# Two masked cross attentions: the masks are made inside the projection block, the mask transfers are issued first, and the position vectors are padded to 128 rows

## The chip, the cores and the metric

One Trainium2 chip, one of its cores. The metric is the device time of one execution of the whole program in microseconds (us). TensorE does matrix products, VectorE (DVE), ScalarE (ACT) and GpSimd (POOL) do elementwise work, SyncE (SP) issues the transfers (DMAs). TensorE's clock has two levels, 1.2 and 2.4 GHz; the profile shows which was granted (0.50 or 1.00).

## The reference

A post-norm decoder of four layers on x of shape (4, 256, 128), thirteen stages one after the other, each followed by `x = layernorm(x + stage(x))`. Two of the stages matter here. Both are cross attentions with 16 heads of 8 features; queries come from x, keys and values from `ctx` (4 x 256 x 128).

```python
# stage L1_xattn: an additive mask
qh, kh, vh = split(x @ wq.T + bq), split(ctx @ wk.T + bk), split(ctx @ wv.T + bv)
score = einsum('bhqd,bhkd->bhqk', qh, kh) / sqrt(8) + mask * -1e9
out = softmax(score) @ vh, heads joined;  return out @ wo.T + bo

# stage L2_xattn: position vectors beside the features, a bias over distance, a boolean mask
sym = (arange(256) % 2)[:, None] * Wsym                   # (256, 64), the same for all batches
query = concat([x, sym], -1) @ Wq + bq                    # 128 + 64 features in
key, value = concat([ctx, sym], -1) @ Wk + bk, concat([ctx, sym], -1) @ Wv + bv
bias = distance_scale * log1p(dist) + parity_strength * (1 - 2 * parity) - dist / exp(localization_length)
logits = where(mask, (query . key + bias) / sqrt(8), finfo.min)
return (softmax(logits) @ value) @ Wo + bo
```

## The kernel before

Activations lie transposed: 128 features in the partitions, 1024 tokens (4 batches of 256) in the free direction, in float32. `decoder` runs the thirteen stages in order.
A masked cross attention is five pieces of work:

1. A mask block. SP fetches the mask and its transpose. In `L1_xattn` DVE scales `mask` by -1e9, ACT scales `maskT`, and POOL clears the buffers `v_heads` and `shiftsT` (`clear_head_buffers`). In `L2_xattn` the pack is waited for and the next pack issued in a block of its own (`weights_in`); then, in the mask block, SP fetches the byte masks `keep` and `keepT`, ACT makes `near`, and DVE makes `sym`, the `bias` (four operations in a chain), and out of the byte masks and the bias `mask` and `maskT`.
2. The projections, `stream(...)`. It takes a list of jobs; job j is a group of products into PSUM bank j modulo 8 on TensorE, and an evacuation by DVE or ACT. A job waits for a free bank only from the ninth on; here there are six. `head_jobs` makes two jobs (two halves of 512 tokens) for q, evacuated by DVE, and two for k, by ACT; `value_jobs` makes two of four 128 x 128 products each, by DVE. In `L2_xattn` each product is followed by a second one that adds `sym` times the `_sym` part of the weights, over 64 rows (partitions), into the same bank.
3. `attention8`, the core: ACT and DVE split q and k in bfloat16 parts, DMAs lay them out by head, TensorE makes scores, and so on. Masks are read here and nowhere earlier.
4. The output product with `add_and_norm`.

A float32 product shows in the trace as two MATMUL records, called pieces here. Line 146 is the product in `stream`, 838 the evacuation of q, 1361 that of k, 1373 that of v, 71 the transfer of a pack.

Of the kernel before, what the change touches and what calls it, by code (L numbers as in the profile page):

```python
# [20 lines left out]
ACT = mybir.ActivationFunctionType  # L21
ALU = mybir.AluOpType
AX = mybir.AxisListType

P = 128
# [95 lines left out]
def stream(K, tag, jobs, banks=8):  # L121
# [9 lines left out]
    with ExitStack() as stack:  # L131
# [18 lines left out]
        @block.scalar  # L150
        def _(act):
            for j, (eng, _, _, evacuate) in enumerate(jobs):
                if eng == "act":
                    act.wait_ge(product_done, j + 1)
                    evacuate(K.bank[j % banks]).then_inc(taken["act"], 1)

        @block.vector
        def _(dve):

            K.chain = Chain(dve, sem("dve_own"))  # L160
            for j, (eng, _, _, evacuate) in enumerate(jobs):
                if eng == "dve":
                    dve.wait_ge(product_done, j + 1)
                    evacuate(K.bank[j % banks]).then_inc(taken["dve"], 1)
# [1213 lines left out]
def L1_xattn(K):  # L1378
# [4 lines left out]
    with ExitStack() as stack:  # L1383
# [5 lines left out]
        with ExitStack() as inner:  # L1389
            sem = Sems(nc, inner, "L1_xattn_mask")  # L1390
            mask_in, cleared = sem("in"), sem("cleared")
            block = inner.enter_context(nc.Block())

            @block.sync
            def _(sp):
                sp.dma_start(mask[:], K.dram["mask_added"]).then_inc(mask_in, 16)
                sp.dma_start(maskT[:], K.dram["mask_addedT"]).then_inc(mask_in, 16)
                weights_wait(K, sp, "L1_xattn")

            @block.gpsimd  # L1400
            def _(pool):
                clear_head_buffers(K, pool, cleared)

            @block.vector
            def _(dve):
                dve.wait_ge(mask_in, 32)
                nc.vector.tensor_scalar(mask[:], mask[:], -1e9, None, ALU.mult)

            @block.scalar
            def _(act):  # L1410
                act.wait_ge(mask_in, 32)
                nc.scalar.activation(maskT[:], maskT[:], ACT.Copy, scale=-1e9)
        group = lambda w, src: lambda g, h: [(W(w)[:, g * P:(g + 1) * P], halves(src)[h])]
        stream(K, "L1_xattn_qkv",
               interleave(head_jobs(K, group("wq", x), W("bq"), q, 1 / math.sqrt(DH8)),
                          head_jobs(K, group("wk", ctx), W("bk"), k, 1.0, "act"))
               + value_jobs(K, lambda c: [(ctx[:, c * P:(c + 1) * P], W("wv"))], W("bv"), v))
# [199 lines left out]
def L2_xattn(K):  # L1617

    nc, x, ctx = K.nc, K.x, K.ctx
    weights_in(K, "L2_xattn")  # L1620
    W = lambda n: K.w("L2_xattn." + n)
    FH = P // 2
    with ExitStack() as stack:
# [7 lines left out]
        sym = sb("sym", [FH, 2 * S])  # L1631
        with ExitStack() as inner:
            sem = Sems(nc, inner, "L2_xattn_mask")
            mask_in, near_done, own = sem("mask_in"), sem("near_done"), sem("dve_own")
            block = inner.enter_context(nc.Block())

            @block.sync
            def _(sp):
                sp.dma_start(keep[:], K.dram["mask_kept"]).then_inc(mask_in, 16)
                sp.dma_start(keepT[:], K.dram["mask_keptT"]).then_inc(mask_in, 16)  # L1640

            @block.scalar
            def _(act):

# [3 lines left out]
            def _(dve):  # L1648
                chain = Chain(dve, own)
                bf = bias[:].rearrange("p c s -> p (c s)")  # L1650
                nc.vector.tensor_scalar(sym[:], W("odd"), W("wsym"), None, ALU.mult)
                chain.link(nc.vector.tensor_scalar(bf, W("log_distance"), W("distance_scale"), None, ALU.mult))
                chain.link(nc.vector.scalar_tensor_tensor(out=bf, in0=W("parity"), scalar=W("parity_strength"), in1=bf,
                                                          op0=ALU.mult, op1=ALU.add))
                dve.wait_ge(near_done, 1)

                chain.link(nc.vector.scalar_tensor_tensor(out=bf, in0=W("distance"), scalar=near[:], in1=bf,
                                                          op0=ALU.mult, op1=ALU.add))
                chain.link(nc.vector.tensor_scalar(bf, bf, 1 / math.sqrt(DH8), None, ALU.mult))
                dve.wait_ge(mask_in, 32)  # L1660

                for m, kept in ((mask, keep), (maskT, keepT)):
                    chain.link(nc.vector.tensor_scalar(m[:], kept[:], 1.0, -MASKED, ALU.subtract, ALU.mult))
                    for b in range(B):
                        mb = m[:, 2 * b:2 * b + 2, :]
                        nc.vector.tensor_tensor(mb, mb, bias[:], ALU.add)
        def group(w, src):
# [3 lines left out]
               interleave(head_jobs(K, group("wq", x), W("bq"), q, 1 / math.sqrt(DH8)),  # L1671
                          head_jobs(K, group("wk", ctx), W("bk"), k, 1.0, "act"))
               + value_jobs(K, lambda c: [(ctx[:, c * P:(c + 1) * P], W("wv")),
                                          (sym[:, (c % 2) * P:(c % 2 + 1) * P], W("wv_sym"))], W("bv"), v))
# [603 lines left out]

def parameters(i):
# [47 lines left out]
    for n in "qk":  # L2327
        w = i["L2_xattn_W" + n][:, by_depth]
        p["L2_xattn.w" + n], p[f"L2_xattn.w{n}_sym"] = w[:P], w[P:]
        p["L2_xattn.b" + n] = column(i["L2_xattn_b" + n][by_depth])  # L2330
    p["L2_xattn.wv"], p["L2_xattn.wv_sym"] = i["L2_xattn_Wv"][:P], i["L2_xattn_Wv"][P:]
    p["L2_xattn.bv"], p["L2_xattn.wo"], p["L2_xattn.bo"] = rows(i["L2_xattn_bv"]), i["L2_xattn_Wo"], column(i["L2_xattn_bo"])
    p["L2_xattn.wsym"] = column(i["L2_xattn_Wsym"])
# [50 lines left out]
    p["L2_xattn.odd"] = np.broadcast_to(np.tile(pos % 2, 2).astype(np.float32), (P // 2, 2 * S))  # L2384
# [43 lines left out]
```

## Time and profile before

| | |
|---|---|
| median of 3 runs | 1736.21 us (1733.26 to 1736.88) |
| the profiled execution | 1738.16 us, its span 1736.3 us |
| mean granted TensorE clock | 0.854 |
| TensorE busy | 1259.2 us, 73% of the span |
| DVE, ACT, POOL busy | 1009.3, 885.4 and 499.7 us |
| stage L1_xattn, first mask transfer to last evacuation of v | 611.98 to 630.48 us |
| stage L2_xattn, next pack's issue to last evacuation of v | 885.31 to 932.20 us |

The profiled execution's own time is 1.9 us above its span (start and end of the program around it). Times inside the trace count from the span's start.

### The profile page before, as it was taken

The page shows a single profiled execution, that of the slowest core. Times are in us where ns is not written, and L with a number is a line of the kernel's source. Part 1 is how long each engine was busy: PE and PEld are TensorE (multiplying, and loading weights), DVE is VectorE, ACT ScalarE, POOL GpSimd, SP SyncE. Part 2 cuts the span into 40 slices and gives each one's busy share as a digit, 9 for nine tenths or more (in the row PEclk, how much of TensorE's full clock was granted, in tenths as well). Part 3 has the DMA queues.
Part 4 walks back from the last instruction along what each step waited for, and adds up shares of the span by engine and source line. Part 5 has one row for each costly group of instructions (what it writes and reads, how often), then busy time and mean ns, then how long its engine had stood idle before and what let it go on. Part 6 is the DMA issues. An engine that isn't in the chain of part 4 may idle for free. (4 is left out here: it accounts for less than half of the span.)

```text
span 1736.3 us, 21579 instructions
## 1 busy us (share of the span) xinstructions
PE 1259.2 (73%) x7168; PEld 628.1 (36%) x7168; DVE 1009.3 (58%) x2042; ACT 885.4 (51%) x1822; POOL 499.7 (29%) x583
## 2 busy tenths in 40 slices
PE   6998645266666749866537996973985979888896
PEld 2575421022222215522213553431433434543462
DVE  2573456999999536413833644442734748736852
ACT  2673234599999546743013772231652564743653
POOL 0362002388888531100302210000200213422440
PEclk9999866589999978978865997975887799989998
DMA  3000000000000034011023400014411500000000
GB/s 136 2 2 2 19 8 0 1 0 0 0 1 0 0 112 90 2 43 37 0 79 66 81 2 35 0 31 107 92 51 37 110 13 39 1 1 1 0 2 13
DMA packets 43486, 52.73 MB, mean 30 GB/s; under 512 B 2800, under 2 KB 39792, under 8 KB 41968
## 3 DMA queue, kind: packets, MB, share of 16 engines
q1 hardware_dynamic: 43376, 51.35, 11.4%
q8 instruction: 58, 0.95, 0.2%
q14 instruction: 52, 0.43, 0.1%
HBM read 36.66 MB, written 14.68 MB: 30 GB/s over the span
## 5 line engine op out<-in xcount | busy, mean ns | idle before, releaser
L1341 POOL TENSOR_TENSOR L_attn_z<-L_attn_state,L_attn_r 128x1024 f32<-128x1024 f32 x64 | 150.8, 2358 | 40.0 <-DVE L_attn_state L1327 33.5
L1327 DVE TENSOR_TENSOR_SCAN L_attn_state<-bank,L_attn_w 128x512 f32<-128x512 f32 x128 | 149.0, 1205 | 0.0
L1238 PE MATMUL bank<-L_attn_z,const 128*128 128x512 f32 x256 | 138.1, 667 | 1.4 <-POOL L_attn_z L1345 1.4
L791 DVE CUSTOM_DVE_ANT_0 L_xattn_core_logits<-bank,L_xattn_mask 128x256 f32<-128x256 f32 x256 | 98.6, 422 | 53.9 <-PE bank L574 41.4
L146 PE MATMUL bank<-x,weights 128*128 128x512 f32 (+1 forms) x108 | 60.0, 711 | 59.6 <-PEq L181 26.1
L1222 PE MATMUL bank<-L_attn_rows,L_attn_select 128*128 128x512 bf16 x96 | 36.9, 442 | 86.1 <-ACT L_attn_C L1290 43.2
L1278 ACT ACTIVATE L_attn_r<-L_attn_after_dt,L_attn_half_guard,L_attn_A 128x512 f32<-128x512 f32 x128 | 96.5, 802 | 0.0
L1268 ACT ACTIVATE bank<-L_attn_dt,L_attn_A 128x510 f32<-128x510 f32 x128 | 86.5, 676 | 13.3 <-DVE L_attn_state L1327 13.3
L703 ACT ACTIVATE L_xattn_core_probs<-bank 128x512 f32<-128x512 f32 x132 | 71.5, 596 | 36.9 <-PE bank L617 25.5
L574 PE MATMUL bank<-L_xattn_core_rows 48*128 48x256 bf16 x384 | 64.6, 312 | 32.2 <-DMA L_xattn_core_rows<-L_xattn_core_slots 18.0
L1345 POOL TENSOR_TENSOR L_attn_z<-L_attn_z,L_attn_C 128x1024 f32<-128x1024 f32 x32 | 75.7, 2367 | 23.7 <-ACT L_attn_C L1290 23.6
L1308 DVE TENSOR_TENSOR L_attn_w<-bank,L_attn_udt 128x1024 f32<-128x1024 f32 x64 | 78.2, 1222 | 5.6 <-PE bank L1222 1.9
L411 POOL TENSOR_TENSOR L_attn_core_probs<-L_attn_core_probs,L_attn_core_rsum 128x256 f32<-128x256 f32 x64 | 51.5, 826 | 93.2 <-DVE L_attn_core_rsum L380 93.2
L1238 PEld LDWEIGHTS bank<-L_attn_z,const 128*128 128x128 f32 x256 | 54.2, 212 | 50.6 <-issue 39.7
L1284 ACT ACTIVATE L_attn_r<-L_attn_r 128x1024 f32<-128x1024 f32 x64 | 66.7, 1043 | 0.0
L2072 PE MATMUL bank<-L_ffn_shifted,weights 128*128 128x512 f32 x128 | 59.1, 606 | 10.0 <-PEq L1999 10.0
L411 POOL TENSOR_TENSOR L_ffn_core_probs<-L_ffn_core_probs,L_ffn_core_rsum 128x256 f32<-128x256 f32 x64 | 51.5, 826 | 45.5 <-DVE L_ffn_core_rsum L380 45.4
L2158 POOL TENSOR_TENSOR L_ffn_part<-L_ffn_part 128x512 f32<-128x512 f32 x32 | 40.8, 1274 | 59.4 <-DVE L_ffn_part L2137 59.4
L761 POOL TENSOR_TENSOR shiftsT<-L_xattn_core_top,nothing 128x8 bf16<-128x8 f32 x48 | 12.0, 251 | 157.6 <-DVE L_xattn_core_top L791 104.6
L602 PE MATMUL bank<-L_xattn_core_rows 48*128 48x256 bf16 x384 | 56.8, 284 | 0.4
L345 ACT ACTIVATE L_ffn_core_probs<-bank,L_ffn_core_negmax 128x128 f32<-128x128 f32 (+1 forms) x128 | 52.0, 426 | 9.2 <-DVE L_ffn_core_negmax L371 9.2
L607 PE MATMUL bank<-L_xattn_core_shifts,minus_rows 48*128 48x256 bf16 x384 | 56.6, 283 | 0.0
(466 smaller groups left out, 3029.9 us busy)
## 6 DMA issues: line engine op xcount, KB each, us to landing
L_xattn_core_rows<-L_xattn_core_slots SPq DMA_DIRECT2D x24, 384.0 KB, 5.8
weights<-in_pack_L_ffn SPq DMA_DIRECT2D x2, 2118.5 KB, 7.9
L_xattn_core_slots<-L_xattn_core_k_parts SPq DMA_DIRECT2D x24, 128.0 KB, 2.0
L_attn_core_rows<-L_attn_core_slots SPq DMA_DIRECT2D x8, 384.0 KB, 5.5
weights<-in_pack_L_ffn SPq DMA_DIRECT2D x1, 2824.0 KB, 9.4
weights<-in_pack_L_attn SPq DMA_DIRECT2D x1, 2304.0 KB, 8.5
L_xattn_core_slots<-L_xattn_core_q_parts SPq DMA_DIRECT2D x12, 192.0 KB, 2.2
weights<-in_pack_L_xattn SPq DMA_DIRECT2D x1, 1539.5 KB, 6.2
```

The lines of the kernel that those rows point to most:

```text
L411: last = nc.gpsimd.tensor_tensor(part, part, rsum[:, i % NB, :, sc:sc + 1].to_broadcast([P, 2, keys[sc].stop]), ALU.mult)
L574: last = nc.tensor.matmul(scores_bank[side][:, c * S:(c + 1) * S], row(QUERIES, side, p, c), row(KEYS, side, p), start=True, stop=True)
L703: nc.scalar.activation(probs[n % 3][:, at], shifted_bank[at][:], ACT.Exp).then_inc(exp_done, 1)
L791: last = nc.vector.tensor_tensor_reduce(logits[:, c], scores_bank[side][:, c * S:(c + 1) * S], mask[:, 2 * b + c, :], 1.0, MASKED, ALU.add ...
L1238: last = nc.tensor.matmul(y_bank[2 * c + half][:], ident, z[:, g % NS, c], start=False, stop=False, skip_group_check=True)
L1268: nc.scalar.activation(two(a_bank[c][:])[:, :, lo:lo + S - 1], two(dt[d][:, c, tokens(half)])[:, :, lo:lo + S - 1], ACT.Exp, scale=A[d][:, ...
L1278: last = nc.scalar.activation(r[:, g % NS, c], after_dt[d][:, c, tokens(half)], ACT.Tanh, bias=half_guard[:], scale=A[d][:, 1, at:at + 1])
L1284: nc.scalar.activation(r[:, g % NS], r[:, g % NS], ACT.Copy, scale=0.5, bias=0.5).then_inc(r_done, 1)
L1308: nc.vector.tensor_tensor(w[:, g % 2], B_bank[:].unsqueeze(1).to_broadcast([P, DC, HALF]), udt[d][:, :, tokens(half)], ALU.mult).then_inc( ...
L1327: nc.vector.tensor_tensor_scan(state[:, g % NS, c, ::step], a_bank[c][:, ::step], w[:, g % 2, c, ::step], 0.0, ALU.mult, ALU.add).then_inc ...
L1341: nc.gpsimd.tensor_tensor(z[:, g % NS], state[:, g % NS], r[:, g % NS], ALU.mult).then_inc(z_done, 1)
L1345: nc.gpsimd.tensor_tensor(z[:, g % NS], z[:, g % NS], copied[:, g // 2 % 2].unsqueeze(1).to_broadcast([P, DC, HALF]), ALU.mult).then_inc(p ...
```

## The change

In `stream` there are three new arguments: `dve_first` puts work at the head of DVE's list of the block, `act_last` at the end of ACT's, `on_pool` gives POOL a list. The scaling of the masks and the clearing of buffers (`L1_xattn`), and the bias and the masks (`L2_xattn`), move there. What is left ahead of the projections in `L1_xattn` is a block in which SP issues three transfers. In `L2_xattn` there are two: one in which SP issues `keep`, `keepT` and then the next stage's pack, and one in which ACT makes `near` and DVE `sym`. In both stages the jobs of k come ahead of those of q. `sym` and the `_sym` weights have 128 rows, of which the upper 64 hold zeros; the packs were already stored with 128 rows, so they keep their sizes.

```diff
-def stream(K, tag, jobs, banks=8):
+def stream(K, tag, jobs, banks=8, dve_first=None, act_last=None, on_pool=None):
...
                     evacuate(K.bank[j % banks]).then_inc(taken["act"], 1)
+            if act_last:
+                act_last(act)
+
+        if on_pool:
+            @block.gpsimd
+            def _(pool):
+                on_pool(pool)
 
         @block.vector
         def _(dve):
 
             K.chain = Chain(dve, sem("dve_own"))
+            if dve_first:
+                dve_first(dve)
             for j, (eng, _, _, evacuate) in enumerate(jobs):
...
 L1_xattn:
-        with ExitStack() as inner:
-            sem = Sems(nc, inner, "L1_xattn_mask")
-            mask_in, cleared = sem("in"), sem("cleared")
-            block = inner.enter_context(nc.Block())
-
+        sem = Sems(nc, stack, "L1_xattn_mask")
+        mask_in, cleared = sem("in"), sem("cleared")
+        with nc.Block() as block:
             @block.sync
             def _(sp):
                 sp.dma_start(mask[:], K.dram["mask_added"]).then_inc(mask_in, 16)
                 sp.dma_start(maskT[:], K.dram["mask_addedT"]).then_inc(mask_in, 16)
                 weights_wait(K, sp, "L1_xattn")
 
-            @block.gpsimd
-            def _(pool):
-                clear_head_buffers(K, pool, cleared)
-
-            @block.vector
-            def _(dve):
-                dve.wait_ge(mask_in, 32)
-                nc.vector.tensor_scalar(mask[:], mask[:], -1e9, None, ALU.mult)
-
-            @block.scalar
-            def _(act):
-                act.wait_ge(mask_in, 32)
-                nc.scalar.activation(maskT[:], maskT[:], ACT.Copy, scale=-1e9)
+        def scale_mask(dve):
+            dve.wait_ge(mask_in, 32)
+            nc.vector.tensor_scalar(mask[:], mask[:], -1e9, None, ALU.mult)
+
+        def scale_maskT(act):
+            act.wait_ge(mask_in, 32)
+            nc.scalar.activation(maskT[:], maskT[:], ACT.Copy, scale=-1e9)
+
...
-               interleave(head_jobs(K, group("wq", x), W("bq"), q, 1 / math.sqrt(DH8)),
-                          head_jobs(K, group("wk", ctx), W("bk"), k, 1.0, "act"))
-               + value_jobs(K, lambda c: [(ctx[:, c * P:(c + 1) * P], W("wv"))], W("bv"), v))
+               interleave(head_jobs(K, group("wk", ctx), W("bk"), k, 1.0, "act"),
+                          head_jobs(K, group("wq", x), W("bq"), q, 1 / math.sqrt(DH8)))
+               + value_jobs(K, lambda c: [(ctx[:, c * P:(c + 1) * P], W("wv"))], W("bv"), v),
+               dve_first=scale_mask, act_last=scale_maskT, on_pool=lambda pool: clear_head_buffers(K, pool, cleared))
...
 L2_xattn:
-    weights_in(K, "L2_xattn")
...
-        sym = sb("sym", [FH, 2 * S])
+        sym = sb("sym", [P, 2 * S])
...
+        with nc.Block() as block:
             @block.sync
             def _(sp):
                 sp.dma_start(keep[:], K.dram["mask_kept"]).then_inc(mask_in, 16)
                 sp.dma_start(keepT[:], K.dram["mask_keptT"]).then_inc(mask_in, 16)
-
+                weights_wait(K, sp, "L2_xattn")
+
+        with nc.Block() as block:
             @block.scalar
             def _(act):
                 nc.scalar.activation(near[:], W("localization_length"), ACT.Exp, scale=-1.0).then_inc(near_done, 1)
 
             @block.vector
             def _(dve):
                 nc.vector.tensor_scalar(sym[:], W("odd"), W("wsym"), None, ALU.mult)
-                chain.link(nc.vector.tensor_scalar(bf, W("log_distance"), W("distance_scale"), None, ALU.mult))
...
+        def make_masks(dve):
+            chain = Chain(dve, own)
+            bf = bias[:].rearrange("p c s -> p (c s)")
+            chain.link(nc.vector.tensor_scalar(bf, W("log_distance"), W("distance_scale"), None, ALU.mult))
...
+            dve.wait_ge(mask_in, 32)
+
+            for m, kept in ((maskT, keepT), (mask, keep)):
+                chain.link(nc.vector.tensor_scalar(m[:], kept[:], 1.0, -MASKED, ALU.subtract, ALU.mult))
+                for b in range(B):
+                    mb = m[:, 2 * b:2 * b + 2, :]
+                    nc.vector.tensor_tensor(mb, mb, bias[:], ALU.add)
...
-               interleave(head_jobs(K, group("wq", x), W("bq"), q, 1 / math.sqrt(DH8)),
-                          head_jobs(K, group("wk", ctx), W("bk"), k, 1.0, "act"))
+               interleave(head_jobs(K, group("wk", ctx), W("bk"), k, 1.0, "act"),
+                          head_jobs(K, group("wq", x), W("bq"), q, 1 / math.sqrt(DH8)))
...
-                                          (sym[:, (c % 2) * P:(c % 2 + 1) * P], W("wv_sym"))], W("bv"), v))
+                                          (sym[:, (c % 2) * P:(c % 2 + 1) * P], W("wv_sym"))], W("bv"), v),
+               dve_first=make_masks)
...
+def all_rows(a):
+    return np.concatenate([a, np.zeros((P - a.shape[0], a.shape[1]), np.float32)])
...
-        p["L2_xattn.w" + n], p[f"L2_xattn.w{n}_sym"] = w[:P], w[P:]
+        p["L2_xattn.w" + n], p[f"L2_xattn.w{n}_sym"] = w[:P], all_rows(w[P:])
-    p["L2_xattn.wv"], p["L2_xattn.wv_sym"] = i["L2_xattn_Wv"][:P], i["L2_xattn_Wv"][P:]
+    p["L2_xattn.wv"], p["L2_xattn.wv_sym"] = i["L2_xattn_Wv"][:P], all_rows(i["L2_xattn_Wv"][P:])
-    p["L2_xattn.wsym"] = column(i["L2_xattn_Wsym"])
+    p["L2_xattn.wsym"] = column(all_rows(i["L2_xattn_Wsym"].reshape(-1, 1)))
-    p["L2_xattn.odd"] = np.broadcast_to(np.tile(pos % 2, 2).astype(np.float32), (P // 2, 2 * S))
+    p["L2_xattn.odd"] = np.broadcast_to(np.tile(pos % 2, 2).astype(np.float32), (P, 2 * S))
```

DVE in stage `L2_xattn`, from the end of the norm before to the evacuations of v. Names are tiles; `L_xattn` stands for the stage, `bank` is a PSUM bank. Before:

```order
L1651 TENSOR_SCALAR L_xattn_sym<-weights 64x512
L1652 TENSOR_SCALAR L_xattn_bias<-weights 128x512
L1653 SCALAR_TENSOR_TENSOR L_xattn_bias<-weights,L_xattn_bias 128x512
L1657 SCALAR_TENSOR_TENSOR L_xattn_bias<-weights,L_xattn_near,L_xattn_bias 128x512
L1659 TENSOR_SCALAR L_xattn_bias<-L_xattn_bias 128x512
L1663 TENSOR_SCALAR L_xattn_mask<-L_xattn_keep 128x2048
L1666 TENSOR_TENSOR L_xattn_mask<-L_xattn_mask,L_xattn_bias 128x512 x4
L1663 TENSOR_SCALAR L_xattn_maskT<-L_xattn_keepT 128x2048
L1666 TENSOR_TENSOR L_xattn_maskT<-L_xattn_maskT,L_xattn_bias 128x512 x4
L1632 UNCONDITIONAL_BRANCH
L157 UNCONDITIONAL_BRANCH
L838 TENSOR_SCALAR L_xattn_q<-bank,weights 128x512 x2
```

The same place with the change (a branch is the step from one block to the next):

```order
L1649 TENSOR_SCALAR L_xattn_sym<-weights 128x512
L1642 UNCONDITIONAL_BRANCH
L164 UNCONDITIONAL_BRANCH
L1654 TENSOR_SCALAR L_xattn_bias<-weights 128x512
L1655 SCALAR_TENSOR_TENSOR L_xattn_bias<-weights,L_xattn_bias 128x512
L1658 SCALAR_TENSOR_TENSOR L_xattn_bias<-weights,L_xattn_near,L_xattn_bias 128x512
L1660 TENSOR_SCALAR L_xattn_bias<-L_xattn_bias 128x512
L1664 TENSOR_SCALAR L_xattn_maskT<-L_xattn_keepT 128x2048
L1667 TENSOR_TENSOR L_xattn_maskT<-L_xattn_maskT,L_xattn_bias 128x512 x4
L1664 TENSOR_SCALAR L_xattn_mask<-L_xattn_keep 128x2048
L1667 TENSOR_TENSOR L_xattn_mask<-L_xattn_mask,L_xattn_bias 128x512 x4
L847 TENSOR_SCALAR L_xattn_q<-bank,weights 128x512 x2
```

The step between blocks moved from behind the masks to behind `sym`; no DVE operation came or went, and q's evacuation still stands behind both masks.

SP in the same stage, before:

```order
L182 UNCONDITIONAL_BRANCH
L71 DMA weights<-in_pack_L_ffn 128x5648
L181 UNCONDITIONAL_BRANCH
L1637 UNCONDITIONAL_BRANCH
L1639 DMA L_xattn_keep<-in_mask_kept 128x2048
L1640 DMA L_xattn_keepT<-in_mask_keptT 128x2048
```

and with the change:

```order
L1636 UNCONDITIONAL_BRANCH
L1638 DMA L_xattn_keep<-in_mask_kept 128x2048
L1639 DMA L_xattn_keepT<-in_mask_keptT 128x2048
L71 DMA weights<-in_pack_L_ffn 128x5648
L1635 UNCONDITIONAL_BRANCH
```

The pack of the next stage now stands behind the two byte masks, and all three are issued in one block.

DVE in stage `L1_xattn`, before:

```order
L1407 TENSOR_SCALAR L_xattn_mask<-L_xattn_mask 128x2048
L1389 UNCONDITIONAL_BRANCH
L157 UNCONDITIONAL_BRANCH
L838 TENSOR_SCALAR L_xattn_q<-bank,weights 128x512 x2
L1373 TENSOR_TENSOR L_xattn_v<-bank,weights 128x512 x2
```

and with the change:

```order
L164 UNCONDITIONAL_BRANCH
L1409 TENSOR_SCALAR L_xattn_mask<-L_xattn_mask 128x2048
L847 TENSOR_SCALAR L_xattn_q<-bank,weights 128x512 x2
L1382 TENSOR_TENSOR L_xattn_v<-bank,weights 128x512 x2
L131 UNCONDITIONAL_BRANCH
```

The scaling of the mask is now behind the step between blocks, at the head of the block that holds the projections.

## Rows read from the trace of the kernel before

**Rows 1.** The page: the span, and busy time by engine.
```profile
span 1736.3 us, 21579 instructions
PE 1259.2 (73%) x7168; PEld 628.1 (36%) x7168; DVE 1009.3 (58%) x2042; ACT 885.4 (51%) x1822; POOL 499.7 (29%) x583
```

**Rows 2.** Timeline, L1_xattn: start, duration, engine, line, operation, count [idle before, releaser].
```profile
610.44 1.29 DVE L247 TENSOR_TENSOR x<-bank,L_attn_norm_inv_std 128x512 f32<-128x512 f32 x2 [4.27 <-ACT L_attn_norm_inv_std L229]
611.98 0.33 SPq L1396 DMA_DIRECT2D L_xattn_mask<-in_mask_added  x1
...
612.84 0.42 SPq L71 DMA_DIRECT2D weights<-in_pack_L_ffn  x1
...
616.26 1.06 POOL L453 MEMSET v_heads<- 128x256 f32 x4
619.21 1.91 ACT L1412 ACTIVATE L_xattn_maskT<-L_xattn_maskT 128x2048 f32<-128x2048 f32 x1 [8.29 <-DMA L_xattn_maskT<-in_mask_addedT]
619.21 1.23 DVE L1407 TENSOR_SCALAR L_xattn_mask<-L_xattn_mask 128x2048 f32<-128x2048 f32 x1 [7.48 <-DMA L_xattn_maskT<-in_mask_addedT]
...
621.41 2.05 PE L146 MATMUL bank<-x,weights 128*128 128x512 f32 x2 [12.25 <-PEq L1389]
...
627.80 1.95 PE L146 MATMUL bank<-weights,ctx 128*128 128x128 f32 x16
...
629.79 0.69 DVE L1373 TENSOR_TENSOR L_xattn_v<-bank,weights 128x512 f32<-128x512 f32 x1 [0.20 <-PE bank L146]
```

**Rows 3.** Timeline, L2_xattn.
```profile
885.31 0.33 SPq L71 DMA_DIRECT2D weights<-in_pack_L_ffn  x1
886.04 0.33 SPq L1639 DMA_DIRECT2D L_xattn_keep<-in_mask_kept  x1
...
886.09 0.48 DVE L1651 TENSOR_SCALAR L_xattn_sym<-weights 64x512 f32<-64x512 f32 x1 [1.03 <-PEq L181]
...
888.57 0.43 DVE L1659 TENSOR_SCALAR L_xattn_bias<-L_xattn_bias 128x512 f32<-128x512 f32 x1
896.09 1.23 DVE L1663 TENSOR_SCALAR L_xattn_mask<-L_xattn_keep 128x2048 f32<-128x2048 uint8 x1 [7.10 <-DMA L_xattn_keepT<-in_mask_keptT]
...
901.02 2.50 DVE L1666 TENSOR_TENSOR L_xattn_maskT<-L_xattn_maskT,L_xattn_bias 128x512 f32<-128x512 f32 x4
...
903.82 2.05 PE L146 MATMUL bank<-x,weights 128*128 128x512 f32 x2 [21.33 <-PEq L1632]
...
905.80 2.07 PE L146 MATMUL bank<-L_xattn_sym,weights 64*128 64x512 f32 x2
...
919.83 0.79 PE L146 MATMUL bank<-weights,ctx 128*128 128x128 f32 x2
...
931.51 0.69 DVE L1373 TENSOR_TENSOR L_xattn_v<-bank,weights 128x512 f32<-128x512 f32 x1 [5.09 <-PE bank L146]
```

**Rows 4.** Windows: stretch, length, busy (records) of PE, PEld, DVE, ACT, POOL; clock.
```profile
903.80:931.50 27.70, 27.65 (x48) 11.98 (x48) 2.19 (x3) 1.37 (x2) 0.00 (x0) 0.50 0.00 1
621.40:627.20 5.80, 5.79 (x7) 2.50 (x8) 1.04 (x2) 0.69 (x1) 0.00 (x0) 0.50 0.00 0
627.20:629.80 2.60, 2.55 (x18) 1.94 (x16) 1.16 (x3) 0.69 (x1) 0.00 (x0) 1.00 0.00 0
...
882.50:903.80 21.30, 0.00 (x0) 0.01 (x1) 11.45 (x17) 1.93 (x4) 0.00 (x0) 0.60 0.41 160
661.00:733.00 72.00, 70.27 (x818) 41.75 (x816) 41.77 (x205) 58.81 (x117) 12.54 (x52) 1.00 0.19 36
```

**Rows 5.** DMA issues: size and median us from issue to landing.
```profile
weights<-in_pack_L_xattn SPq DMA_DIRECT2D x1, 321.5 KB, 2.8
...
L_xattn_keepT<-in_mask_keptT SPq DMA_DIRECT2D x1, 256.0 KB, 9.6
```

**Rows 6.** Timeline, PE alone: 128-column pieces at 0.50, 512-column pieces at 1.00.
```profile
212.19 3.62 PE L146 MATMUL bank<-const,L_ffn_ints 128*128 128x128 f32 x16
...
634.23 3.70 PE L559 MATMUL bank<-x,const 128*128 128x512 f32 x8 [1.47 <-DVE L_xattn_core_q_parts L778]
```

More of the change, by code:

```diff
@@ L1619, in L2_xattn @@
     nc, x, ctx = K.nc, K.x, K.ctx
-    weights_in(K, "L2_xattn")
     W = lambda n: K.w("L2_xattn." + n)
-    FH = P // 2
     with ExitStack() as stack:
@@ L1630, in L2_xattn @@
         bias, near = sb("bias", [P, 2, S]), sb("near", [P, 1])
-        sym = sb("sym", [FH, 2 * S])
[L1632 to L1635, printed above, removed]
+        sym = sb("sym", [P, 2 * S])
+        sem = Sems(nc, stack, "L2_xattn_mask")
+        mask_in, near_done, own, sym_done = sem("mask_in"), sem("near_done"), sem("dve_own"), sem("sym_done")
+        with nc.Block() as block:
             @block.sync
@@ L1648, in _ @@
             def _(dve):
-                chain = Chain(dve, own)
-                bf = bias[:].rearrange("p c s -> p (c s)")
                 nc.vector.tensor_scalar(sym[:], W("odd"), W("wsym"), None, ALU.mult)
-                chain.link(nc.vector.tensor_scalar(bf, W("log_distance"), W("distance_scale"), None, ALU.mult))
[L1653 to L1666, printed above, removed]
+        def make_masks(dve):
+            chain = Chain(dve, own)
+            bf = bias[:].rearrange("p c s -> p (c s)")
+            chain.link(nc.vector.tensor_scalar(bf, W("log_distance"), W("distance_scale"), None, ALU.mult))
+            chain.link(nc.vector.scalar_tensor_tensor(out=bf, in0=W("parity"), scalar=W("parity_strength"), in1=bf,
+                                                      op0=ALU.mult, op1=ALU.add))
+            dve.wait_ge(near_done, 1)
+            chain.link(nc.vector.scalar_tensor_tensor(out=bf, in0=W("distance"), scalar=near[:], in1=bf,
+                                                      op0=ALU.mult, op1=ALU.add))
+            chain.link(nc.vector.tensor_scalar(bf, bf, 1 / math.sqrt(DH8), None, ALU.mult))
+            dve.wait_ge(mask_in, 32)
[4 more added lines that the diff above has]
+                    nc.vector.tensor_tensor(mb, mb, bias[:], ALU.add)
         def group(w, src):
```

## The prediction

> **What bounds the kernel now.** I read the page first. TensorE is busy for 73% of the span and no engine is near all of it [rows 1], so shares decide nothing; what counts is which wait ends last in the two stages that the change touches. Then the timelines of both, from the end of the norm before to the last evacuation of v.
>
> In L1_xattn [rows 2] the norm ends at 610.44 + 1.29 = 611.73. SP issues three transfers from 611.98 to 612.84 + 0.42 = 613.26. DVE and ACT wait for both masks until 619.21, and scale them until 620.44 and 621.12. TensorE starts at 621.41, having been idle for 12.25 us, its releaser a block step (PEq); POOL had been done at 617.32. It ends at 627.80 + 1.95 = 629.75, and the last v is out at 629.79 + 0.69 = 630.48. The reader is to see that the products use neither mask nor cleared buffer; they wait only because they stand in the next block.
>
> In L2_xattn [rows 3] the same wait is longer. The next pack is issued at 885.31, `keep` at 886.04. The transposed mask lands 9.6 us after its issue [rows 5]; DVE, done with the bias at 888.57 + 0.43 = 889.00, stands until 896.09 and makes masks until 901.02 + 2.50 = 903.52. TensorE starts at 903.82 after 21.33 us idle; the last v is out at 931.51 + 0.69 = 932.20.
>
> Third, the windows with the clock [rows 4]. L2's projections, 903.80 to 931.50, are 48 pieces in 27.70 us, TensorE busy for 27.65 of them, and the clock is at 0.50 (1.2 GHz) throughout. L1's 24 pieces began at 0.50 too, but after 5.80 us the clock went to 1.00, and the rest took 2.55 us. L1 has only products over 128 rows; in L2 every second one is over 64 [rows 3].
>
> **L1_xattn, step by step.** The block ahead of the products ends when SP has issued its third transfer, 613.26. A step from an SP issue to the next block takes 886.09 - (885.31 + 0.33) = 0.45 us [rows 3]. So TensorE starts at 613.7. At the same length as now (8.35 us, if the clock rises as late as now) it ends at 622.05. DVE's first instruction in that block is the scaling, which waits for the DMA as now: 619.21 + 1.23 = 620.44. Queued behind it are two evacuations of q and two of v, each 128x512 like the v row at 0.69: 623.2. TensorE doesn't wait for them, since six jobs fit in eight banks. ACT: k's evacuations end before the mask lands, then maskT until 621.12. POOL's clearing took from 612.2 to 617.3, so 5.1 us; from 613.7 it ends at 618.8, behind the projections and free, and would cost only past 623.2. The stage's last evacuation moves from 630.48 to 623.2: **7.2 us less**. The limit is then the mask's landing plus DVE's queue; k before q changes nothing, as ACT takes k while DVE is at the mask.
>
> **L2_xattn, the start.** SP now issues three transfers in a row in the first block. In L1 three took 613.26 - 611.98 = 1.28 us [rows 2], so 885.31 + 1.28 = 886.6; one block step, 0.45, gives 887.05; `sym`, 0.48, gives 887.5 (zeros in 64 more partitions run beside the others, so I take the same time); a step from DVE's last operation to TensorE is 903.82 - 903.52 = 0.3. TensorE starts at 887.8 instead of 903.82: 16.0 us.
>
> **L2_xattn, the products.** 16 pieces of 512 columns and 32 of 128. Now the 128-row pair at 903.82 is followed at 905.80: 0.99 per piece. L1, at the same clock, did 5.80 us / 6.8 pieces = 0.85. The remaining 32 take (931.50 - 919.83) / 32 = 0.365 each, where full-row 128-column pieces at 0.50 take 3.62 / 16 = 0.226 [rows 6]. So alternating 128 and 64 rows costs some time at the same clock: all 48 at the full-row prices are 16 x 0.85 + 32 x 0.226 = 20.8 us, 6.9 less than 27.7. If the clock also rises after 5.8 us, as in L1, then 6.8 pieces are done by then, the other 9.2 take at most 3.70 / 8 = 0.46 each [rows 6], 4.2 us, and the 32 take L1's 1.95 / 16 = 0.122 [rows 2], 3.9 us: 13.9 us, another 6.9 less. I take this: L1's stretch has the same pieces, starts after a similar idle time at 0.50, and differs only in the rows. TensorE ends at 887.8 + 13.9 = 901.7, v is out at 902.5, **29.7 us less** than 932.20.
>
> Whether DVE keeps up: from 887.8, the bias (889.00 - 886.57 = 2.4) until 890.2, both masks (903.52 - 896.09 = 7.4) until 897.6, q until 899.0, v's first half by 899.7; it waits for the second, with 2.0 us to spare. `keepT` must land by 890.2 + 2.0. Alone in the queue, a 321.5 KB transfer landed in 2.8 us [rows 5]; two of 256 KB one behind the other are at best in at 888.1, at worst at 885.3 + 5.6 = 890.9. No cost either way. The next pack, now third, is wanted a whole stage later; by today's 9.6 us it is in by about 897, before the core's own transfers begin. If it were still moving then, its rest would lie on the core's path.
>
> One page speaks against the padding. First the rows: 0.99 beside 0.85 per piece and 0.365 beside 0.226 [rows 2 to 4, 6]. The Trainium skill, "TensorE: Matmul & The Clock Gate", section "Why this matters for your kernels", states that a single product over 32 rows takes the same time as one over 128. By that, filling up rows buys nothing, and the sum would be the third case below; the trace disagrees for a mixture of the two heights. The same page, Part 1, says that sustained TensorE work lifts the clock, and names no row count. By that the stage before should have risen as well; the trace disagrees, 27.7 us of nearly full busy time at 0.50. So something else may hold it there, and that is the second case.
>
> **The sum.** 7.2 + 29.7 = 36.9. The profiled span 1736.3 becomes 1699.4. Its execution was 1738.16, 2 us above the median of the runs, 1736.21; I take the difference off the median: 1736.2 - 36.9 = 1699.3 us.
>
> **Rivals.**
>
> 1. As summed, 1699. For it: L1's clock. 76 in 100. Its own range is 1695 to 1703. The clock was at 1.00 for a fifth of the 21.3 us idle window (mean 0.60) [rows 4], so it fell near 886.8, one microsecond before the new start. If it doesn't fall, TensorE needs 16 x 0.46 + 3.9 = 11.3 us, DVE's queue ends last at 900.4, and the time is 1697. The runs of before spread by 3.6 us.
> 2. The padding removes the alternation but the clock stays at 0.50: TensorE 887.8 to 908.6, v out at 909.4, gain 22.8 + 7.2 = 30.0: 1706. For it: 27.7 us in which the clock did not move. 12 in 100.
> 3. The padding does nothing: 27.7 us from 887.8, v out at 916.2, gain 16.0 + 7.2 = 23.2: 1713. Against it: the piece prices. 6 in 100.
> 4. The byte masks still land as late as now (896.0, say if the queue doesn't serve in order of issue): masks at 903.4, four evacuations to 906.2, 3.7 us of the gain lost: 1703. Against it: `keep`, issued behind the pack, landed behind it. 3 in 100, inside the range.
> 5. Slower: the cores lose the high clock. L1's ran at 1.00 from 661 to 733 with TensorE busy for 70.3 of 72 us [rows 4]; at 0.50 that work would take twice as long, so 37 us of it at the lower level would eat the whole gain, and both cores' would give 1736 + 103 at worst. What could do it is a core that begins after a different stretch of products. Against it: L1's core already follows full-row products at 1.00, and L2's will now do the same. 2 in 100, with 1 in 100 for a partial loss that ends near no change.
>
> **Chances and range.** 3.5 us (0.2%) is about what a measurement can tell here from no change. Cases 1 to 4 are all faster, 97 in 100. The range holds cases 1, 2 and 4: 1695 to 1707.
>
> **What would show it.** In the trace after: TensorE's first piece in L1 at about 613.7 and in L2 about 16 us sooner than 903.8, less what L1 gave; the scaling of L1's mask still at 619.2 and v's last evacuation there right behind DVE's queue; in L2 `keepT` landing within 5 us; the 512-column pieces first at 0.85 and then below 0.46, with the clock at 1.00 some 6 us after the start. I am wrong if the window of L2's projections stays at 0.50, if pieces stay at 0.99, or if a stage that was not touched changed by more than 2 us.

## The result and the profile after

The changed kernel took 1697.92 us (median of 4 runs, 1697.51 to 1698.12) beside 1735.11 us: ratio 0.9784, 95% interval 0.9772 to 0.9796. The forecast was 1699.3 us, range 1695 to 1707. Run again in a later session beside the kernel before, it took 1699.20 us (1696.00 to 1701.34, 5 runs; ratio 0.9782, 0.9766 to 0.9798). The first profiled execution took 1697.51 us, its span is 1695.6 us.

The page, the span and busy time by engine, to be held beside [rows 1] (PE is TensorE's products, PEld its weight loads):

```profile
span 1695.6 us, 21581 instructions
PE 1237.5 (73%) x7160; PEld 621.3 (37%) x7168; DVE 1008.9 (59%) x2042; ACT 885.5 (52%) x1822; POOL 500.5 (30%) x583
```

DVE, ACT and POOL did the same work as before, to within 1 us. TensorE is busy for 21.7 us less with the same number of instructions (of its matmul records, 8 are missing from the second trace). 14.2 us of it lie in L2's projections (27.65 before, 5.58 + 7.89 after, windows below): a faster clock, and pieces that start closer behind each other. The rest of the gain is idle time.

Timeline of L1_xattn after, against [rows 2] (line numbers moved: 1403 and 1404 issue the masks, 1409 and 1413 scale them, 847, 1370 and 1382 evacuate q, k and v):

```profile
610.57 1.29 DVE L256 TENSOR_TENSOR x<-bank,L_attn_norm_inv_std 128x512 f32<-128x512 f32 x2 [4.27 <-ACT L_attn_norm_inv_std L238]
612.11 0.33 SPq L1403 DMA_DIRECT2D L_xattn_mask<-in_mask_added  x1
...
612.97 2.03 SPq L71 DMA_DIRECT2D weights<-in_pack_L_ffn  x1
...
615.44 2.05 PE L146 MATMUL bank<-ctx,weights 128*128 128x512 f32 x2 [6.15 <-PEq L1400]
...
620.43 1.23 DVE L1409 TENSOR_SCALAR L_xattn_mask<-L_xattn_mask 128x2048 f32<-128x2048 f32 x1 [8.57 <-DMA L_xattn_maskT<-in_mask_addedT]
...
621.46 1.95 PE L146 MATMUL bank<-weights,ctx 128*128 128x128 f32 x16
...
622.89 1.28 DVE L1382 TENSOR_TENSOR L_xattn_v<-bank,weights 128x512 f32<-128x512 f32 x2
```

Count from the end of the norm, 611.86 here and 611.73 before. The last v was out 18.75 us after it and is now out after 12.31 (624.17): 6.44 us less, where 7.2 was forecast. TensorE idles for 6.15 us instead of 12.25. But SP's third issue took 2.03 us instead of 0.42, and the masks were in 1.1 us later (DVE's idle 8.57, before 7.48). More on that below.

Timeline of L2_xattn after, against [rows 3]:

```profile
877.07 1.29 DVE L256 TENSOR_TENSOR x<-bank,L_attn_norm_inv_std 128x512 f32<-128x512 f32 x2 [5.03 <-ACT L_attn_norm_inv_std L238]
878.61 0.33 SPq L1638 DMA_DIRECT2D L_xattn_keep<-in_mask_kept  x1
...
879.47 0.42 SPq L71 DMA_DIRECT2D weights<-in_pack_L_ffn  x1
...
880.34 0.49 DVE L1649 TENSOR_SCALAR L_xattn_sym<-weights 128x512 f32<-128x512 f32 x1 [1.98 <-PEq L1635]
881.12 2.05 PE L146 MATMUL bank<-ctx,weights 128*128 128x512 f32 x2 [5.33 <-PEq L1642]
...
882.96 1.91 PE L146 MATMUL bank<-L_xattn_sym,weights 128*128 128x512 f32 x2
...
883.69 1.23 DVE L1664 TENSOR_SCALAR L_xattn_maskT<-L_xattn_keepT 128x2048 f32<-128x2048 uint8 x1
...
888.62 2.50 DVE L1667 TENSOR_TENSOR L_xattn_mask<-L_xattn_mask,L_xattn_bias 128x512 f32<-128x512 f32 x4
...
891.03 1.40 DVE L847 TENSOR_SCALAR L_xattn_q<-bank,weights 128x512 f32<-128x512 f32 x2
...
894.63 0.69 DVE L1382 TENSOR_TENSOR L_xattn_v<-bank,weights 128x512 f32<-128x512 f32 x1 [1.09 <-PE bank L146]
```

The norm ends at 878.36 here (885.05 before). The last v is out 895.32 - 878.36 = 16.96 us later; before it was 932.20 - 885.05 = 47.15. That is 30.19 us less; 29.7 was forecast. The masks wait for no transfer any more (the row at 883.69 has no releaser). DVE waits for TensorE again at the last v, by 1.09 us, so TensorE is what bounds the stretch and DVE's queue hides beside it.

The windows of L2's projections after, against [rows 4] (stretch, length, busy of PE, PEld, DVE, ACT, POOL, clock), and the DMA issues, against [rows 5]:

```profile
881.10:886.70 5.60, 5.58 (x7) 2.51 (x8) 5.40 (x8) 0.69 (x1) 0.00 (x0) 0.50 0.99 368
886.70:894.60 7.90, 7.89 (x42) 5.27 (x41) 6.39 (x10) 0.69 (x1) 0.00 (x0) 1.00 0.30 122
```

```profile
weights<-in_pack_L_ffn SPq DMA_DIRECT2D x1, 2824.0 KB, 13.1
L_xattn_keep<-in_mask_kept SPq DMA_DIRECT2D x1, 256.0 KB, 2.7
L_xattn_keepT<-in_mask_keptT SPq DMA_DIRECT2D x1, 256.0 KB, 3.0
```

5.6 us at 1.2 GHz, then 2.4 GHz: 13.5 us where 27.7 stood. `keepT` landed 3.0 us after its issue instead of 9.6. The pack behind it took 13.1 us and was in at 892.6, before the core's first transfer.

### The profile page after: what moved, and what is told of

It is laid out like the page before. It is cut to its first block and busy times, and to the rows that moved or that the text cites. A ratio compares the mean times of both kernels' runs of the same rounds, so it can differ in the third digit from the quotient of the medians.

```text
span 1695.6 us, 21581 instructions
## 1 busy us (share of the span) xinstructions
PE 1237.5 (73%) x7160; PEld 621.3 (37%) x7168; DVE 1008.9 (59%) x2042; ACT 885.5 (52%) x1822; POOL 500.5 (30%) x583
## 5 line engine op out<-in xcount | busy, mean ns | idle before, releaser
L1247 PE MATMUL bank<-L_attn_z,const 128*128 128x512 f32 x256 | 138.1, 667 | 1.7 <-POOL L_attn_z L1354 1.4
L712 ACT ACTIVATE L_xattn_core_probs<-bank 128x512 f32<-128x512 f32 x132 | 71.6, 596 | 36.9 <-PE bank L626 25.4
## 6 DMA issues: line engine op xcount, KB each, us to landing
L_xattn_core_slots<-L_xattn_core_k_parts SPq DMA_DIRECT2D x24, 128.0 KB, 2.0
weights<-in_pack_L_ffn SPq DMA_DIRECT2D x1, 2824.0 KB, 13.1
```

The source lines that it names most:

```text
L712: nc.scalar.activation(probs[n % 3][:, at], shifted_bank[at][:], ACT.Exp).then_inc(exp_done, 1)
L1247: last = nc.tensor.matmul(y_bank[2 * c + half][:], ident, z[:, g % NS, c], start=False, stop=False, skip_group_check=True)
```

## The experiments

Each ran beside the kernel before on the same chip; medians of 3 to 5 runs. Where a stage is given, it is the time from the end of one norm to the end of the next in the profiled execution:

| kernel | median us | ratio (95%) | L1_xattn | L2_xattn | all behind it |
|---|---|---|---|---|---|
| before | 1735.1 to 1735.8 | | 136.5 | 162.0 | 686.0 |
| changed | 1697.92 | 0.9784 (0.9772 to 0.9796) | 129.8 | 132.9 | 681.1 |
| changed, again | 1699.20 | 0.9782 (0.9766 to 0.9798) | 128.0 | 133.9 | 683.6 |
| padding alone | 1723.71 | 0.9926 (0.9910 to 0.9943) | 136.6 | 148.3 | 686.0 |
| all but the padding | 1715.58 | 0.9884 (0.9867 to 0.9900) | 129.7 | 148.1 | 686.1 |
| L1_xattn alone | 1728.69 | 0.9955 (0.9939 to 0.9972) | 128.1 | 163.9 | 681.0 |
| pack first in L2 | 1702.89 | 0.9817 (0.9801 to 0.9834) | 129.0 | 138.1 | 682.5 |
| 128-row products first, no padding | 1705.06 | 0.9813 (0.9796 to 0.9831) | 129.9 | 136.2 | 681.3 |
| 64-row products first, no padding | 1706.67 | 0.9827 (0.9812 to 0.9842) | 128.1 | 139.8 | 680.9 |
| pack and small steps moved | 1693.76 | 0.9761 (0.9746 to 0.9775) | 126.6 | 131.1 | 679.6 |

Read the column of L1_xattn with care. The code of the stage behind it is the same everywhere, yet it took 42.1 to 42.2 us where L1_xattn took 129.7 to 129.9, and 43.8 us where L1_xattn took 128.0 to 128.1. Together the two stages took 178.6 us before and 171.8 to 172.0 in six of the seven traces in which L1_xattn is as in the changed kernel (172.8 in the seventh, the pack first; 168.7 with the small steps moved). So L1's part of the change is worth 6.6 to 6.8 us, whether its own column shows 6.6 or 8.5.

**1. The padding alone.** The kernel before, with

```diff
-        sym = sb("sym", [FH, 2 * S])
+        sym = sb("sym", [P, 2 * S])
...
-        p["L2_xattn.w" + n], p[f"L2_xattn.w{n}_sym"] = w[:P], w[P:]
+        p["L2_xattn.w" + n], p[f"L2_xattn.w{n}_sym"] = w[:P], all_rows(w[P:])
```

and the like for v, `wsym` and `odd`.

> The kernel before with one part of the change alone: sym and the _sym weights filled up to 128 rows. If the rows are what holds the clock (my theory), L2's 48 projection pieces take about 14 us instead of 27.7, the clock reaches 1.00 some 6 us after their start, and the time falls by 13.8 us to about 1721 (ratio 0.992). If the alternation of heights only costs time per piece and the clock stays at 0.50: 20.8 us of pieces, 6.9 us gained, about 1728. If one product over 64 rows takes as long as one over 128 and nothing else hangs on it: no change, 1735.

Measured: 1723.71 us, the stage 13.7 us shorter. The windows of its 48 pieces:

```profile
904.70:907.80 3.10, 3.08 (x4) 1.50 (x5) 0.00 (x0) 0.00 (x0) 0.00 (x0) 0.51 0.02 5
907.80:916.90 9.10, 9.09 (x45) 5.82 (x43) 2.19 (x3) 1.37 (x2) 0.00 (x0) 1.00 0.00 0
```

12.2 us instead of 27.7. The start is where it was, after 21.6 us of idle time, so neither the idle time before nor the work beside held the clock. It rose 3.1 us after the start here and 5.6 in the changed kernel, with the same pieces; that moment varies. The medians differ by 11.4 us where 13.8 was expected and the stage gave 13.7; both kernels' runs spread by over 4 us, and the interval of the ratio, 0.9910 to 0.9943, is 9.9 to 15.6 us.

**2. All but the padding.** The changed kernel with the 64-row forms back.

> The changed kernel with sym and the _sym weights over 64 rows again. By my sum the pieces take 27.7 us at clock 0.50 and the whole is 13.8 us slower than the changed kernel, about 1712 (ratio to the kernel before 0.987). A rival: since DVE is at work beside the products now and TensorE starts only about 5 us after its last work, the clock could rise all the same; then the pieces take 16 to 20 us and the time is about 1703. If the padding is worth nothing, 1698.

```profile
880.70:908.40 27.70, 27.65 (x48) 11.98 (x48) 11.88 (x17) 1.38 (x2) 0.00 (x0) 0.50 0.28 109
```

The same 27.7 us at 0.50 as before, to the record, though TensorE had been idle for 5.3 us and not 21.3. 1715.58 us, 3.6 above the 1712 that was expected; in the traces the stretch behind L2_xattn, which the padding doesn't touch, took 5.0 us more than in the changed kernel's first. In the stage the two halves of the change add up. Moved work took it from 162.0 to 148.1, padding alone from 162.0 to 148.3, which is 27.5 us together; both at once took it to 132.9 and 133.9, 29.1 and 28.1 us less.

**3. L1_xattn alone.** `stream` and `L1_xattn` of the changed kernel, `L2_xattn` of the one before.

> The change in stage L1_xattn alone, L2_xattn as before. The stage in the changed kernel's trace is 6.8 us shorter (136.5 to 129.8), so about 1728.5 (ratio 0.996); 7.2 was predicted. If the masks' landing were hidden anyway and only the trace's clock pattern differed, under 2 us. SP's third DMA issue is looked at too: 2.03 us in the changed kernel, 0.42 before. If that belongs to the new order it is about 2 us again; if it is chance, about 0.4, and the stage comes out another 1 us shorter at most.

1728.69 us, as expected. In the trace the third issue took 0.42 us, and the stage was 1.7 us shorter than in the changed kernel's first profile; the stage behind it took 1.6 us more, so the end of the two came no sooner.

**4. The pack first.** In L2's first block:

```diff
+                weights_wait(K, sp, "L2_xattn")
                 sp.dma_start(keep[:], K.dram["mask_kept"]).then_inc(mask_in, 16)
                 sp.dma_start(keepT[:], K.dram["mask_keptT"]).then_inc(mask_in, 16)
-                weights_wait(K, sp, "L2_xattn")
```

> The changed kernel, but in L2_xattn the next stage's pack is issued ahead of keep and keepT again. If the queue serves in order of issue, keepT lands about 9.6 us after its issue, DVE makes the masks about 5 to 6 us later than in the changed kernel, and the last v is out about 3.7 us later: about 1701.5 (ratio 0.9805). If the transfers share the engines evenly, keepT lands within 4 us and the time is the changed kernel's, 1698.

1702.89 us. The DMA issues and DVE's wait of this kernel:

```profile
L_xattn_keepT<-in_mask_keptT SPq DMA_DIRECT2D x1, 256.0 KB, 10.9
```

```profile
885.44 1.23 DVE L1664 TENSOR_SCALAR L_xattn_maskT<-L_xattn_keepT 128x2048 f32<-128x2048 uint8 x1 [6.84 <-DMA L_xattn_keepT<-in_mask_keptT]
...
894.10 1.28 DVE L1382 TENSOR_TENSOR L_xattn_v<-bank,weights 128x512 f32<-128x512 f32 x2
```

Both byte masks land only about when the 2.8 MB ahead of them do: 10.5 us after its issue the pack, 9.6 and 10.9 us after theirs `keep` and `keepT`. TensorE had ended at 889.5; DVE, late by the transfer, ended at 895.38 with masks and all four evacuations in a row. The norm had ended at 873.30, so the last v is out after 22.08 us, 5.1 later than in the changed kernel. Expected were 3.7: 0.9 us of the difference is that `keepT` landed 1.3 us later after its issue than before (10.9, not 9.6), the rest that the changed kernel had its v out 0.5 us sooner than forecast. The stage is 4.2 to 5.2 us longer than in the changed kernel's two traces, and the median 3.7 to 5.0 above its two. So the order of the transfers is worth about 4 to 5 us here, not because masks are needed soon but because DVE's queue has four evacuations behind them.

**5. The 128-row products first.** Without padding; TensorE takes the q and k jobs in two passes, and v's jobs stay as they were:

```diff
+            for k in range(2 if grouped else 0):
+                for j in range(grouped):
+                    (at, n, pairs), = jobs[j][2]
+                    last = nc.tensor.matmul(K.bank[j][0:jobs[j][1], at:at + n], pairs[k][0], pairs[k][1],
+                                            start=(k == 0), stop=(k == 1))
...
```

> The changed kernel without the padding, and TensorE takes the four products over 128 rows of the q and k jobs first, then their four over 64 rows; v's alternate as before. If the cost per piece comes from each change of height, the 16 pieces of 512 columns take 0.85 each at clock 0.50 instead of 1.00. If 64-row pieces are what keeps the clock down, it rises about 6 us after the start, during the last 128-row pieces, and falls again in the 64-row ones; projections of 18 to 24 us, time 1704 to 1711. If alternating is what keeps it down, it rises and stays through the 64-row pieces: about 16 us or less, time near 1702.

**6. The 64-row products first.** The same with `for k in (1, 0)`.

> As the run before, but the four products over 64 rows come first. If 64-row pieces keep the clock down, it is at 0.50 through all eight of them (6.8 us) and rises only about 6 us into the 128-row pieces, or not before v's alternation starts; if it is the alternation, it rises about 6 us after the start as in the padded kernel, in the 64-row pieces or right behind them, and the time is near 1702.

The windows of experiment 5 (eight 128-row pieces until 887.9, eight 64-row pieces, then v alternating):

```profile
881.40:887.00 5.60, 5.55 (x7) 2.49 (x8) 5.37 (x8) 0.00 (x0) 0.00 (x0) 0.50 1.09 450
887.00:891.40 4.40, 4.40 (x10) 1.46 (x9) 4.37 (x8) 1.37 (x2) 0.00 (x0) 0.99 0.28 118
891.40:898.20 6.80, 6.80 (x33) 4.73 (x32) 2.05 (x4) 0.01 (x1) 0.00 (x0) 1.00 0.00 0
```

and of experiment 6 (eight 64-row pieces until 889.4, then the 128-row ones):

```profile
882.30:889.40 7.10, 7.03 (x8) 2.50 (x8) 6.86 (x10) 0.00 (x0) 0.00 (x0) 0.50 0.96 349
889.40:894.90 5.50, 5.50 (x8) 2.34 (x8) 3.67 (x6) 0.69 (x1) 0.00 (x0) 0.51 0.23 99
894.90:902.30 7.40, 7.38 (x35) 4.90 (x33) 1.44 (x2) 0.69 (x1) 0.00 (x0) 1.00 0.00 0
```

The medians are 1705.06 us (experiment 5) and 1706.67 (experiment 6). These two separate what the padding did at once. In experiment 6 nothing alternates for 7.1 us, TensorE has no gap, and the clock stays at 1.2 GHz; it rises only 5.5 us after the first 128-row piece. In experiment 5 it rises 5.6 us after the 128-row pieces began, and then 64-row pieces (3.70 us for eight) and the alternating ones do not bring it down. So 64-row pieces did not lift the clock here, and did not lower it. One of the cases put down for experiment 5 had it fall again in the 64-row pieces; it did not. The case in which alternating keeps the clock down fits experiment 5 and is refuted by experiment 6.

That the moment of the rise varies does not spoil this reading. In six traces the clock fell 1.2 us before L2's first piece, to the same tenth. In four of them full-height pieces followed (both of the changed kernel, experiments 4 and 5), and each time it rose 5.6 us after the first. With the mixture (experiment 2) it did not rise in 27.7 us, and with 64-row pieces first (experiment 6) it rose after 12.5. It is still one execution of each of these two kernels.

The alternation has its own price, and experiment 6 shows what carries it:

```profile
882.37 7.16 PE L142 MATMUL bank<-L_xattn_sym,weights 64*128 64x512 f32 x8 [5.33 <-PEq L1651]
...
884.21 0.33 PEld L142 LDWEIGHTS bank<-L_xattn_sym,weights 64*128 64x128 f32 x1 [0.52 <-issue]
...
885.06 0.33 PEld L142 LDWEIGHTS bank<-L_xattn_sym,weights 64*128 64x128 f32 x1 [0.52 <-issue]
...
889.46 2.07 PE L142 MATMUL bank<-ctx,weights 128*128 128x512 f32 x2
...
891.33 1.91 PE L142 MATMUL bank<-x,weights 128*128 128x512 f32 x2
...
893.03 1.91 PE L142 MATMUL bank<-ctx,weights 128*128 128x512 f32 x2
```

Between 64-row pieces in a row, piece follows piece (and weight load follows weight load) after 0.85 us, exactly as between 128-row pieces (893.03 - 891.33 = 1.70 for two). Height as such costs nothing. What costs is the change: the last piece ahead of it and the first behind it take 0.13 and 0.16 us more (891.33 - 889.46 = 1.87 for two). With 24 products of alternating height there are 23 changes, and 23 x 0.29 = 6.7 us; that is an estimate from this one change at 1.2 GHz, and it comes close to the 6.9 us that the forecast put on the spacing. At 2.4 GHz v's alternating pieces take 6.8 / 32 = 0.21 us each, padded ones 0.11 (two pieces from 890.86 to 891.08 in the changed kernel). The rows of the weight loads hint at why. This is the load for the second product, in the changed kernel and in the kernel before:

```profile
882.11 0.34 PEld L146 LDWEIGHTS bank<-L_xattn_sym,weights 128*128 128x128 f32 x1 [0.52 <-issue]
```

```profile
905.80 0.50 PEld L146 LDWEIGHTS bank<-L_xattn_sym,weights 64*128 64x128 f32 x2 [1.50 <-issue]
```

The first began 0.85 us ahead of its piece (882.96), beside the piece before it. The second, where the height changed, began together with its piece (905.80). That the load is hidden in one case and not in the other is read from this, not tested.

Grouping without any padding recovers 11.9 of the 15.2 us that the padding gave the stage (148.1 to 136.2, and to 132.9).

**7. Pack and small steps moved.** The changed kernel, with the next pack issued inside the projection block, `sym` and `near` made in the block that issues the masks, and L1's q evacuated ahead of the mask's scaling:

```diff
+        if on_sync:
+            @block.sync
+            def _(sp):
+                on_sync(sp)
...
             @block.vector
             def _(dve):
+                dve.wait_ge(K.loaded, 16 * (K.stages.index("L2_xattn") + 1))
                 nc.vector.tensor_scalar(sym[:], W("odd"), W("wsym"), None, ALU.mult)
```

> The changed kernel with the next stage's pack issued inside the projection block in both stages, sym and near made in the same block in which the masks are issued, and in L1_xattn q evacuated ahead of the mask's scaling. If what stands ahead of TensorE is SP's issues and a block step, its first piece comes 1 to 2.5 us sooner in L1 and about 1.3 us sooner in L2; L1's end is set by the mask's landing and gains about 1 us. Together 2 to 3 us below the changed kernel, near 1695.5. If the instruction load beside the mask transfers, seen in L1 (1.7 us), only moves to another place, under 1 us.

1693.76 us, 5.4 below the changed kernel in the same session, and the fastest version of this study. The runs of the two just overlap (1691.38 to 1696.50, 1696.00 to 1701.34), and so do the intervals of their ratios. Its timeline:

```profile
612.39 0.33 SPq L1414 DMA_DIRECT2D L_xattn_mask<-in_mask_added  x1
...
613.67 1.74 PE L146 MATMUL bank<-ctx,weights 128*128 128x512 f32 x2 [4.10 <-PEq L1411]
...
875.52 0.33 SPq L1650 DMA_DIRECT2D L_xattn_keep<-in_mask_kept  x1
...
876.81 2.05 PE L146 MATMUL bank<-ctx,weights 128*128 128x512 f32 x2 [4.11 <-PEq L1647]
```

From the first mask issue to TensorE's first piece it is 1.28 us in L1 (3.33 in the changed kernel, 1.73 in its second profile) and 1.29 in L2 (2.51). The two stages are 1.4 to 3.2 and 1.8 to 2.8 us shorter than in the two profiles of the changed kernel: 4.1 to 4.9 together, more than the 2 to 3 expected. With the stage behind L1_xattn counted in, L1's part is 3.2 to 3.3. Four things were moved at once, and nothing was run that tells them apart.

**8. The changed kernel again.**

> The changed kernel once more, for a second profile and beside the run before. 1697.9 us as measured; stages L1_xattn 129.8 and L2_xattn 132.9 us. If the 4 to 5 us that its first trace gained behind L2_xattn belong to the change, they come again; if they are the clock's pattern of one execution, they differ by some us.

1699.20 us. Its timeline of L1, with the norm's end at 612.20:

```profile
613.31 0.42 SPq L71 DMA_DIRECT2D weights<-in_pack_L_ffn  x1
...
614.18 2.04 PE L146 MATMUL bank<-ctx,weights 128*128 128x512 f32 x2 [4.54 <-PEq L1400]
...
619.70 1.23 DVE L1409 TENSOR_SCALAR L_xattn_mask<-L_xattn_mask 128x2048 f32<-128x2048 f32 x1 [7.50 <-DMA L_xattn_maskT<-in_mask_addedT]
```

The same program: the third issue takes 0.4 us, TensorE starts 1.98 us after the norm (forecast 1.97), the masks land as before the change. So the long issue does not belong to the new order as such. The DMA view of the first profile, 611 to 622 us, has what differs:

```profile
q1 hardware_dynamic: 432, 2.37, 57.8%
q8 instruction: 1, 0.02, 1.0%
```

One packet of instructions, 16 KB, started 0.1 us after the third issue's start and took 1.76 us beside 2 MB of masks; in the second profile, in the kernel before and in experiment 3 no instruction packet lies beside the masks. In experiments 2 and 4 one starts 0.1 us into the third issue again, and that issue took 1.99 and 1.89 us. In experiment 5 one starts 0.5 us after the third issue has ended; the issue took 0.42 us, but `maskT` landed 8.4 us after its own, not 6.8, and the last v was out after 12.84 us. So a packet beside the masks goes with a later landing (in all four traces), and with a long issue only where it starts inside it. That it is the cause is what this suggests; nothing was run that moves it on purpose. Its cost doesn't last: over L1_xattn and the stage behind it the changed kernel's two traces took 171.9 and 171.8 us, with and without it. The stretches behind L2_xattn, whose code is the same in all ten traces, took 679.6 to 686.1 us; the second profile of the changed kernel 2.5 us more than the first. So the first trace's extra gain of 4.9 us there is not the change's alone.

## Why the prediction was right

**The bound** held. In both stages TensorE waited for work that its products did not use, and starts earlier by what was forecast: 2.76 us behind the norm in L2 (forecast 2.75), and in L1 1.98 in the second profile (forecast 1.97), though 3.58 in the first, with its long issue.

**L1's term**, 7.2 us. 6.44 in the first profile; in the second the last v is out at 622.16 + 1.28 = 623.44, 11.24 us behind the norm, 7.5 less than before. What set it was as said, the masks' landing and DVE's queue; that the masks could land a microsecond later, as in the first profile, was not foreseen. Of either, 6.7 to 6.8 us are left at the end of the stage behind.

**L2's start**, 16.0 us: 13.8 us of the stage by experiment 2, where TensorE's first piece came 16.0 us sooner after the norm (880.75 - 877.99 = 2.76 instead of 18.77) and the stretch from the last v to the norm's end, whose code is the same, took 117.0 us where it had taken 114.8. **L2's products**, 13.8 us: 27.7 to 13.5 us in the changed kernel, to 12.2 with the padding alone. The rise after 5.8 us was 5.6. Of the split in two times 6.9, the half for the pieces' spacing is borne out by the price of one change of height in experiment 6 (23 of them, 6.7 us); the half for the clock was not measured by itself. One reading under it was wrong: the forecast took the clock's rise from L1's stretch, which "starts after a similar idle time", but that was 12.25 us, and L2's is 5.33 now. The clock had fallen all the same, 1.2 us ahead of the first piece; the forecast gave it one microsecond, and had it not fallen the time would have been near 1697, within the range.

**DVE's slack** of 2.0 us was 1.09. The price of losing the early masks, 3.7 us in rival 4, measured 5.1: that number took the landing time of the kernel before, and the transfer was 1.3 us slower.

**What was luck.** The forecast is 36.9 us of gain and the medians gave 37.2, but not from the stages alone. In the traces L1_xattn with the stage behind it gave 6.7 and 6.8 us and L2_xattn 29.1 and 28.1, together 35.8 and 34.9; behind L2_xattn, where the forecast had nothing, came another 4.9 and 2.4. And one of the forecast's own signs of being wrong came: "if a stage that was not touched changed by more than 2 us". The stage right behind L2_xattn took 91.9 us before and 88.6 after. It was a poor sign, as the same program took 91.0 there in its second profile, and experiment 3, in which L2_xattn is untouched too, 88.3. It shows all the same that untouched stages are worth some us either way, for which the sum had no term.

**Rows, and what lifts the clock.** The Trainium skill, "TensorE: Matmul & The Clock Gate", section "Why this matters for your kernels", says that a single product over 32 rows takes as long as one over 128. The trace of experiment 6 agrees for 64-row pieces in a row (0.85 us, as 128-row ones) and not for the mixture (0.99). Part 1 of the page names sustained work as what lifts the clock; 7.1 us of back-to-back 64-row pieces did not, in the one trace that has them. The measurement decides. Rival 3 (the padding does nothing) and rival 2 (it removes the alternation alone) both fell with experiment 1, where padding by itself took the pieces from 27.7 to 12.2 us at a clock that rose.

Rivals 4 and 5 did not occur: `keepT` landed in 3.0 us, and in the trace after the cores kept their clock: that of L1_xattn 1.00 from 655 to 729 us, that of L2_xattn 0.94 on average from 915 to 990.

## What to carry to other kernels

A block that only prepares operands should hold nothing but what the next instructions read; ask of each of its parts who reads it first, and let the rest run beside that reader's predecessors. Small transfers that somebody waits for go ahead of a large one that nobody needs yet, and what it costs if they don't is read at the end of the queue behind the waiting instruction (5.1 us in experiment 4), not at the wait. Where TensorE is busy and its clock still low, look at the rows of its operands: padding to 128, which cost no bytes here because the packs had that height already, or putting the full products first, both let it rise. And if products of two heights must be mixed, change the height as seldom as possible.

## What the runs showed that I had not expected

The clock, once at 2.4 GHz, stayed there through eight 64-row pieces and 32 alternating ones (10.3 us, 887.8 to 898.1 in experiment 5), while alternating pieces did not lift it in 27.7 us, nor eight 64-row ones in 7.1. Pieces over 64 rows cost as much as those over 128, and a change between the two 0.29 us at 1.2 GHz. An instruction packet of 16 KB fell beside a large transfer in one execution of a program and not in the next; where it did, the transfer landed 1.1 to 1.6 us later, and where it started inside an issue on SP, that issue took 1.5 to 1.6 us longer. Code that was untouched took up to 6.5 us more or less, depending on the kernel and the execution, so a trace's span differences are worth less than its stages'; and a stage's own end can be off by 1.7 us that the next stage gives back.
